# A waiting schedule for GpSimd's table gathers in a DLRM tower kernel

## The reference

```python
e = stack([tbl_f[ids[:, f]] for f in range(32)], axis=1)    # 512 x 32 x 64, float32
# every pair i < j of the 32 fields, 496 pairs
z[b, p] = sum_jj (e[b, i, :] @ w[p])[jj] * e[b, j, jj]       # w: 496 x 64 x 64
h = concatenate([z, dense_ctx], axis=1)                      # 512 x 512
h = maximum(h @ W_top1 + b_top1, 0)                          # 512 x 512
h = maximum(h @ W_top2 + b_top2, 0)                          # 512 x 256
y = h @ W_top3                                               # 512 x 1
```

## Time and profile before

| | |
|---|---|
| device time, median of 3 runs | 280.09 us |
| lowest and highest run | 278.54, 280.71 us |
| profiled execution: span | 271.9 us |
| profiled execution: its own device time | not recorded |
| TensorE busy | 212.6 us (78%) |
| VectorE, ScalarE, GpSimd busy | 175.2, 151.6, 150.5 us |

### The profile page before, as it was taken

The page is one execution under the profiler, slowest core; times in us unless marked ns, Lnnn a source line. Parts: engine busy times, 40 slices in busy tenths (PEclk is TensorE's granted clock), DMA queues, the critical chain, the costliest instruction groups (busy, mean ns, idle before and its releaser), DMA issues.

```text
span 271.9 us, 7232 instructions
## 1 busy us (share of the span) xinstructions
PE 212.6 (78%) x2584; PEld 146.7 (54%) x2584; DVE 175.2 (64%) x160; ACT 151.6 (56%) x1146; POOL 150.5 (55%) x186
## 2 busy tenths in 40 slices
PE   0236200899789789799799979789998999999995
PEld 0025100365546376466458647466756786667884
DVE  0000100779676867688698776687897798989741
ACT  1100000256686779277963882926796497899601
POOL 4777773546564635455465644465662683677600
PEclk9999555599999999999999999999999999999999
DMA  6568776601010100101011010011110000000000
GB/s 186 180 185 275 226 227 203 254 17 29 19 28 16 27 15 18 22 17 24 18 19 22 22 27 12 14 27 21 24 25 13 19 4 4 2 1 1 2 2 3
DMA packets 9893, 15.29 MB, mean 56 GB/s; under 512 B 3073, under 2 KB 3329, under 8 KB 9730
## 3 DMA queue, kind: packets, MB, share of 16 engines
q1 hardware_dynamic: 5762, 10.63, 11.6%
q0 software_dynamic: 4096, 4.20, 8.0%
HBM read 14.82 MB, written 0.00 MB: 54 GB/s over the span
## 4 chain that ended last, share of the span: by engine, by line
PE 69%; another core or an unknown queue 11%; issue 9%; DVE 5%; POOL 2%; DMA 2%; ACT 1%; DVEq 0%
PE pu L488 22%; PE pu L496 21%; PE pz L513 13%; PE pt L520 4%; DVE turned L397 3%; PE pt L463 3%; PE pt L532 3%; POOL emb L290 2%; DVE prod L415 2%; DMA emb<-in_tbl,idx 1%; PE pu L520 1%; PE pt L542 1%; DMA idx<-in_ids 1%; PE pt L474 1%
## 5 line engine op out<-in xcount | busy, mean ns | idle before, releaser
L290 POOL DMA_INDIRECT emb<-in_tbl,idx x128 | 121.1, 946 | 94.6 <-PE pu L488 38.6
L318 ACT ACTIVATE turned<-turned 128x64 f32<-128x64 f32 x544 | 130.3, 245 | 2.4 <-DVE turned L397 1.5
L318 ACT ACTIVATION_READ_ACCUMULATOR turned<-turned 128x1 f32 x544 | 103.9, 191 | 0.5 <-issue 0.5
L415 DVE TENSOR_TENSOR prod<-pu,eT 128x1024 f32<-128x1024 f32 x48 | 57.4, 1218 | 49.1 <-issue 29.1
L397 DVE TENSOR_TENSOR turned<-pu,emb 128x1024 f32<-128x1024 f32 x64 | 75.9, 1216 | 17.1 <-PE pu L488 17.0
L496 PE MATMUL pu<-eT,ws 64*128 64x128 f32 x1024 | 71.7, 283 | 10.5 <-issue 9.1
L496 PEld LDWEIGHTS pu<-eT,ws 64*128 64x128 f32 x1024 | 65.0, 192 | 22.8 <-issue 20.9
L488 PE MATMUL pu<-ws,eT 64*128 64x512 f32 x256 | 69.1, 634 | 2.5 <-DVE prod L415 2.1
L309 ACT COPY eT<-pt 128x128 f32<-128x128 f32 (+1 forms) x28 | 11.2, 401 | 81.5 <-PE pt L463 40.9
L513 PE MATMUL pz<-prod,select 128*32 128x128 f32 x1024 | 40.6, 276 | 11.4 <-issue 10.8
L513 PEld LDWEIGHTS pz<-prod,select 128*32 128x32 f32 x1024 | 29.5, 110 | 24.8 <-issue 20.0
(11 more groups left out here) (24 smaller groups left out, 25.6 us busy)
## 6 DMA issues: line engine op xcount, KB each, us to landing
ws<-in_w SPq DMA_DIRECT2D x32, 256.0 KB, 3.5
emb<-in_tbl,idx POOLq DMA_INDIRECT x128, 2.4
w1s<-in_w SPq DMA_DIRECT2D x1, 1024.0 KB
zT<-in_dense SPq DMA_DIRECT2D x1, 512.0 KB
w2s<-in_w SPq DMA_DIRECT2D x1, 512.0 KB
idx<-in_ids SPq DMA_DIRECT2D x1, 64.0 KB, 1.8
identity<-in_ident SPq DMA_DIRECT2D x1, 64.0 KB, 2.4
w3s<-in_w SPq DMA_DIRECT2D x1, 1.0 KB
```

The lines of the kernel that those rows point to most:

```text
L290: nc.gpsimd.indirect_dma_start(out=emb[:, c % EC, x, :], out_offset=None, in_=tables[x], in_offset=bass.IndirectOffsetOnAxis(ap=idx[:, c, ...
L318: i = nc.scalar.activation(t, t, ACT.Copy, accum_out=zB[:, b // NT % 2, b % NT * 16 + v:b % NT * 16 + v + 1])
L415: nc.vector.tensor_tensor(p.rearrange("p x s b -> p x (s b)"), u.rearrange("p x s b -> p x (s b)"), e, ALU.mult).then_inc(mult_done, 1)
```

## The change

The waits of GpSimd ahead of the gathers of the first two chunks are changed; those of the third and fourth chunk stay as they were. In chunk 0 gathers 0 to 15 still wait for nothing. Gathers 16 to 31 wait for as many steps of products as the transposition step of their pair less two: 4, 6, 7, 10, 11, 12, 14 and 21 for pairs 8 to 15. In chunk 1 gather x waited for x + 1 steps (1 to 32); now it waits for 18 + 25x/32, rounded down (18 to 42).

```diff
+GATHERS_FREE = 16
+GATHER_FROM, GATHER_STEPS = 18, 25
+
+def gather_after(c, x):
+    if c == 0:
+        return max(0, X_AT[0][x // 2] - 2) if x >= GATHERS_FREE else 0
+    if c == 1:
+        return GATHER_FROM + x * GATHER_STEPS // FIELDS
+    return (c - 1) * NU + x + 1
...
             for c in range(BCH):
                 for x in range(FIELDS):
-                    if c:
-                        pool.wait_ge(u_ready, (c - 1) * NU + x + 1)
+                    if gather_after(c, x):
+                        pool.wait_ge(u_ready, gather_after(c, x))
                     if c >= EC and x == 0:
                         pool.wait_ge(mult_done, (c - EC + 1) * NU)
```

## The result

The changed kernel takes 294.49 us (median of 4 runs, 292.41 to 297.56); the kernel before took 280.32 us (median of 4). The ratio is 1.051, 95% interval [1.046, 1.057]: 5% slower, where 4% faster was forecast. The profiled execution of the changed kernel took 292.41 us with a span of 290.5 us, so what lies around the span is 1.9 us and not the 8.2 us that the prediction carried. If before has 1.9 us around its span as well, the execution of before whose profile was shown took 273.8 us, an estimate, and was some 6 us quicker than the median run.

The account below looks back on a forecast made before the run. It took the kernel to be bound by TensorE completions held by weight-block traffic until about 48.5 us, then by TensorE. Span 271.9 - 16.6 + 5.2 = 260.5, plus 8.2 around it: 268.7 us, 4.1% less; range 261 to 287.

Parts of the forecast that it names:

- What bounds the kernel now: Reading of the profile before: TensorE's completions held until about 48.5 us by the weight-block stream, then a TensorE-bound 223 us.
- part 2: First chunk from the 17th gather: its wait stops GpSimd and the stream, completions are free at 32.0, 16.6 us go.
- Part 3: First chunk's pairs 8 to 15: late landings cost 5.1 us, less 2 us for slack, so 3 us remain.
- given back: First chunk: 2 us taken off the 5.1 us of lateness, a choice, because TensorE was ahead of VectorE.
- L of 3.3: Time from a gather's issue to its landing, taken as 3.3 us; the page's median was 2.4.
- Part 4: Second chunk: ten gathers behind the 32nd make the first group's transposition 2.2 us late; the next group is on time.
- Chunk 2's gathers start some 11 steps late and gain 0.5 us a step: Third chunk, counted from 0: its first group is used 15 steps after its gathers start; cost put at nothing.
- GpSimd has idle time in every later turn: Claim on GpSimd's queue that the waits as instructions cost nothing.
- Rival C: Stall returns in pieces as the postponed 12 blocks and 16 gathers meet TensorE at work; 276.7 us, chance 0.22.
- Rival A: Start: the stall stays, ending near 48.5 us whatever is issued later; 285.3 us, chance 0.20.
- Rival B: Start: the stall belongs to the profiled execution alone, TensorE held by the writing of its records; 285.3 us, chance 0.06.
- The base: Whole kernel: profiled span of 271.9 us, with 8.2 us around it carried unchanged to the median of 280.09.

Follow-up runs that it names:

- late_traffic: Kernel before with 24 more 256 KB weight-block DMAs into an unread spare tile from step 60 on; ratio 1.002.
- one_burst: Kernel before with the third chunk's first gathers waiting for 46 steps, so that 14 go back to back; 291.66 us against 276.16.
- change_again: The changed kernel run once more, unedited, in a set without holds; 231.22 us against 217.31 for the kernel before.
- paused_again: Kernel before with GpSimd clearing a spare tile after each first-chunk gather from the ninth on, set without holds; 231.75 us against 217.31.
- second_chunk_alone: Kernel before with the changed waits of the second chunk alone, first chunk's gathers free, set without holds; ratio 1.008.
- even_gates: Changed kernel with the first chunk's last pair waiting for 15 steps and later chunks' gathers for evenly rising steps; 279.77 us, 1.4% slower than before.

## Why the prediction was wrong

The step that failed is in "What bounds the kernel now" and part 2: the stall was put down to the stream of weight blocks because it lay over it in time. Over the same time lay the 33 gathers without a gap, and the prediction had that row and read it as the pump of the stream. Traffic alone holds nothing (late_traffic, 210 GB/s, ratio 1.002), gathers alone do (one_burst, 24 GB/s, 15.5 us slower).

Part 2's number: 16.6 us expected to go, 21.9 went. GpSimd's stop at 22.7 did end the hold, for the other reason, and that the change moved both at once was luck. The direction was right and the term was too small, since the hold ended 2.8 us after the last gather and not 3.5 us after the last landing.

Part 3: 3 us lost in the first chunk, and 3.2 measured between steps 1 and 21 (35.1 us against 31.9) in the execution with holds. The size was right, in part by luck. In the changed kernel's trace TensorE waits for a pair at four places, 6.1 us in all against the 5.1 of the prediction: 1.67 us for pair 9 (1.8 forecast), 0.59 for pair 10 (1.2), 1.37 for pair 12 (2.1 for pairs 12 and 13), and 2.42 for pair 14, which was put at nothing. Its gathers went at 49.68 and 50.93 and the pair landed at 54.49, with TensorE at that place from 52.2 on. The 2 us "given back" were a choice, and 2.9 came.

L of 3.3 was sound: the two landings in the chain of that trace from 25 to 60 us take 2.76 and 3.56 us. These are the landings in the chain of change_again, in a set without holds (start us, us, what):

```profile
21.74 4.16 DMA emb<-in_tbl,idx
...
32.88 3.55 DMA emb<-in_tbl,idx
...
43.84 3.58 DMA emb<-in_tbl,idx
...
66.95 2.51 DMA emb<-in_tbl,idx
```

They take 3.45 us on average. The estimate of 2.1 us for L by the Trainium skill, DMA: Bandwidth & Descriptors, section on the anatomy of one DMA, is below all four.

Part 4: 2.2 us expected. It named the ten gathers that stand behind the 32nd and counted their time as lateness; what it missed is that a run of nine (and, for the chunk after, of 14) is itself a hold. "Chunk 2's gathers start some 11 steps late and gain 0.5 us a step", which was put at nothing, is the most expensive sentence of it: those gathers are the second hold, 13.9 us. Where there are no holds, parts 3 and 4 together are 13.9 us and not 5.2: steps take 1.46 us on average there (185 us over 127 steps), against 1.25 us for a gather, so GpSimd has next to no lead at the start and each pause of it reaches TensorE, 7.3 us in the first chunk and as much at the second chunk's first group. "GpSimd has idle time in every later turn" was true of the execution with holds alone.

Rival C (the stall comes back in pieces) is nearest to what happened, but with the wrong carrier and a third of the price (8 us, where the two new holds cost 24.4). Rival A's time of 285 was for a stall that stays. Rival B isn't settled. The prediction's argument against it, that the timed runs would be shorter than the span, doesn't hold: each timed run has its span recorded, so no run here was without recording. What speaks for B is that the traces of the two kinds differ in their records: for kernels with all 128 gathers, those with holds keep 815 to 1167 records of semaphore landings, those without 2627 to 2681. Which is cause and which effect, they don't say. The Trainium skill's NOTIFIC — Programmer's Manual, programming model, allows a record queue to stall its producer as well as to drop. No run here shows whether that is what holds TensorE, nor why it does so in four sets and not in two.

The base was read wrongly too: 1.9 us lie around the span, not 8.2; the rest is that the profiled execution of before was a quick one. The forecast doesn't suffer from it, since span and 8.2 us make up the median, but the ledger does: 18.6 us between the two profiled executions are 14.2 between the medians.

## What to carry to other kernels

When an engine's completions are held and nothing in the profile is named for it, list everything that starts and ends with the hold and move one of them alone to a quiet place; two short kernels did here what no reading of the overlap could. A wait that relieves one place makes a backlog in an in-order queue, so follow the queue until it has caught up and ask what its burst does there. And take the free rate of the queue before pausing it: here 128 gathers at 1.25 us are 160 us of a 217 us kernel, and 15 us of pause ahead of the second chunk's first group cost 14 us (change_again, paused_again).

## What the runs showed that was not expected

The same kernel took 276 to 280 us in four sets of runs and 217 us in two; why is open. In the first kind TensorE passes a few matmuls each 1.4 to 2.1 us (one or two in one_burst, up to five in the changed kernel's first new hold) while GpSimd issues gathers without a gap, from about the fourth of them until some 3 to 5 us after the last; at the start of before, though, the matmuls of steps 0 and 1 ran at their ordinary pace from 19.11 on, with the run of gathers long under way. A pause of 0.6 us a gather nearly ends the hold. In the second kind runs of 96 and 98 gathers leave TensorE busy 90% and 87% of the span (second_chunk_alone, change_again). No even pacing beat the kernel before in the first kind (even_gates 1.4% slower), and in the second none of the versions that compute the whole result did.
